# Another slot table for the side work of an attention kernel: two fills in one step, flags and values of a group later, norms' exponential one step earlier

## The chip, the cores and the metric

The kernel runs on one core of one Trainium2 chip. The metric is device time in microseconds of one execution, as the median of several runs. The profile is one further execution, recorded by the hardware.

## What is computed

Input is x of 8 batches x 1024 tokens x 256 features, and the layer has 16 heads of 16. Its reference, cut down:

```
x = x + attn(layernorm(x));  x = x + ffn(layernorm(x))
def attn(x):
    q, k, v = split_heads(x @ W_q.T), split_heads(x @ W_k.T), split_heads(x @ W_v.T)
    q_h, k_h, v_h = exp_map_at_origin(q, c), exp_map_at_origin(k, c), exp_map_at_origin(v, c)
    diff = |q_h|^2 - 2 q_h.k_h + |k_h|^2
    arg = maximum(1 + 2 c diff / ((1 - c |q_h|^2) (1 - c |k_h|^2)), 1 + EPS)
    weights = softmax(-beta * arccosh(arg) / sqrt(c) - bias)
    out = weights @ log_map_at_origin(v_h, c)
    out = log_map_at_origin(exp_map_at_origin(out, c), c)
    return concat_heads(out) @ W_o.T
def ffn(x):          # bfloat16 in; x and kernel rounded to float8_e4m3
    return bf16(f8(x / s_in) @ f8(kernel / s_k) * s_in * s_k) + bias
```

For each pair of a query and a key there is one logarithm and one power, 134 million of each (8 x 16 x 1024 x 1024).

## The kernel before

**Groups and steps.** The 8192 tokens are 16 groups of 512 query tokens (two groups per batch). For one group and one head group (4 of the 16 heads), the keys of the batch are run through in 8 tiles of 128. Such a piece is a step; a group has 32 steps (s = 0 to 31), the whole kernel 512 (n). In a step TensorE makes the `distances` of 128 keys x 512 queries x 4 heads as products of rows of 18 numbers (q_T, k_T) into four PSUM banks, ScalarE takes a logarithm of them (`log`, L1217) and an exponential of that (`power`, L1224), and TensorE multiplies by the values (`values`, into bank 6). Some groups of steps are "open": flags tell that a bound may be missed, and VectorE then computes and clamps (L1285, L1294). TensorE works ahead: in iteration n it issues the second half of the distances of step n+1 and the first half of n+2 (eight instructions, L1100), then side work, then the values of n-1, then more side work.

**Side work.** Besides the steps each group of tokens is projected once, two groups ahead, and finished once, one group after its steps. The projection of a group (`project_stage`) reads x, normalises it (xt), turns it (X, 2 fills), multiplies by the weights (M, 8 fills, L401), squares and sums q, k, v, finds 1/norm with Newton rounds (L267 to L269), takes the norms' exponential on ScalarE (L529), makes the values (L598 to L604), scales the rows of queries and keys, turns them (R, 8 fills, L406) and makes the flags from their largest norms (A, 2 fills, L411 to L414, then L509 to L521 on VectorE). The finish of a group (`finish_stage`) turns its sums (T, W, L695), and after the second normalisation does the feed-forward product (Q, Y, L700, L706). The sums of each head group are turned too (S, `turn_sums`, at s = 2, 10, 18, 26).

**Bank 7.** Every fill of this side work goes through PSUM bank 7: TensorE fills it, VectorE (in a few places another engine) copies it away, and only then comes the next fill. TensorE waits for `b7_copied` ahead of a fill, VectorE for `b7_filled` ahead of a copy. What follows the waiting fill in TensorE's order waits with it.

**Order.** The place of each piece is written out in tables. `PROJECT_USES` and `FINISH_USES` give for each fill a slot and a half of the step (0 ahead of the values, 1 behind, `BOTH` split). Slot k of the projection of group n is step s = k - 4 of group n - 2 (slots 0 to 3 are steps 28 to 31 before it; group 2's are a little different, `SECOND_USES`; groups 0 and 1 are projected ahead of the steps and in the first steps, `FIRST_FILLS` and `FIRST_USES`). Slot k of the finish is step k of the group after. `vector(v, n, k)` of both stages holds VectorE's work of a slot; in a step VectorE does the copies of bank 7 first, then `copy_sums` (at s = 0, 8, 16, 24; L1300), then the slot work of the finish, then that of the projection. `project.scalar` holds the exponential. Steps without a fill get a dummy product on bank 7 (`keep_busy`, L1138), except step `BARE`. Every fourth step is a new unit: each engine loads a flag and branches to the open or closed form of four steps. SyncE issues the DMAs of a slot in its own order.

**Table before, per step** (of groups 1 to 13): X0 0, X1 1, S 2, M0 3, M1 4, M2 5, M3 6, bare 7, M4 8, M5 9, S 10, M6 11, M7 12, T0 13, T1 14, W0 15, W1 17, S 18, R0 21, R1 22, R2 and A0 23, R3 24, R4 25, S 26, R5 and A1 27, R6 28, R7 29, Q0 30, Y0 and Y1 31.

## Time and profile before

| | us |
|---|---|
| median of 3 runs | 1992.56 |
| lowest and highest | 1990.39, 1993.75 |
| the profiled execution | 1994.49 |
| its span | 1992.7 |
| a regular group of 32 steps, by its first logarithms | 115.13 |
| the first group | 137.96 |

The page gives for each engine its busy time: ScalarE 1869.9 us (94%), TensorE 1788.6 (90%), VectorE 1142.9 (57%). In the rows below, "PE" is TensorE, "PEld" its weight loads, "DVE" VectorE, "ACT" ScalarE. A row of the timeline begins with its start; "[0.50 <-PE ps L700]" behind it says that the engine stood idle 0.50 us ahead of it and what ended that. Two ScalarE instructions that follow each other overlap a little, so that the durations are longer than the distance of the starts (1.78 us).

### The profile page before, as it was taken

The numbers are of one execution on the slowest core, as the hardware profiler recorded it, in microseconds if no ns is written. First come the engines' busy times: TensorE is split into PE (matmuls) and PEld (weight loads), VectorE is DVE, ScalarE is ACT, GpSimd is POOL, SyncE is SP. The second block draws the span as 40 slices with busy tenths as digits, with TensorE's granted clock in tenths as the row PEclk, the third lists the DMA queues.
The fourth block names the chain that finished last, engine by engine and source line by source line (L and its number), as shares of the span: only waits on it lengthen the run. The fifth ranks groups of instructions, "written<-read, shape, count | busy, mean of one in ns | idle before, by whom it ended". The sixth has DMA issues, their size and how long they took to land.

```text
span 1992.7 us, 29554 instructions
## 1 busy us (share of the span) xinstructions
PE 1788.6 (90%) x10713; PEld 603.1 (30%) x10713; DVE 1142.9 (57%) x2825; ACT 1869.9 (94%) x1094; POOL 12.8 (1%) x35
## 2 busy tenths in 40 slices
PE   7988989989898798989998898998989899899897
PEld 4322222323232232322322223232322223233234
DVE  7454565655656656565656647565565656323436
ACT  4889999999999799999998999999999999999883
POOL 2000000000000000000000000000000000000000
PEclk9799999999999899999999899999999999999889
DMA  1314213141312213132040321314131131411110
GB/s 56 112 49 144 54 54 103 42 134 43 112 44 78 77 44 112 43 101 75 23 134 22 110 67 44 112 43 134 40 107 52 56 90 43 123 43 53 33 33 23
DMA packets 112953, 142.54 MB, mean 72 GB/s; under 512 B 35691, under 2 KB 61548, under 8 KB 112748
## 3 DMA queue, kind: packets, MB, share of 16 engines
q1 hardware_dynamic: 112748, 140.13, 22.6%
q8 instruction: 89, 1.46, 0.3%
q14 instruction: 116, 0.95, 0.2%
HBM read 85.07 MB, written 55.05 MB: 70 GB/s over the span
## 4 chain that ended last, share of the span: by engine, by line
ACT 54%; PE 24%; issue 14%; DVE 4%; ACTq 3%; DMA 0%; DVEq 0%; SPq 0%
ACT U L1217 28%; ACT U L1224 26%; PE ps L1100 8%; PE ps L401 6%; PE ps L1115 5%; ACTq L1265 2%; PE ps L695 2%; DVE U L1294 1%; PE ps L1138 1%; PE ps L406 1%; PE ps L1142 1%; DVE U L1285 1%; DVE rows L554 0%; DMA U<-in_L_attn_W_o_dram 0%; ACT e L529 0%
## 5 line engine op out<-in xcount | busy, mean ns | idle before, releaser
L1224 ACT ACTIVATE U<-U 128x2048 f32<-128x2048 f32 x512 | 997.1, 1949 | 0.3
L1217 ACT ACTIVATE U<-ps 128x2048 f32<-128x2048 f32 x500 | 955.7, 1911 | 35.5 <-PE ps L1100 31.6
L1100 PE MATMUL ps<-q_T,k_T 18*128 18x512 f32 x4096 | 632.5, 652 | 133.0 <-ACT U L1217 107.7
L1115 PE MATMUL ps<-U,vals 128*32 128x512 f32 x4096 | 560.4, 620 | 29.4 <-ACT U L1224 28.9
L1100 PEld LDWEIGHTS ps<-q_T,k_T 18*128 18x128 f32 x4096 | 195.9, 187 | 356.8 <-ACT U L1217 296.4
L401 PE MATMUL ps<-wT,xnT 128*128 128x384 f32 x512 | 232.0, 545 | 4.9 <-DVEq L1318 2.5
L490 DVE COPY qkv<-ps 128x384 f32<-128x384 f32 x112 | 62.4, 557 | 243.7 <-PE ps L401 243.6
L1115 PEld LDWEIGHTS ps<-U,vals 128*32 128x32 f32 x4096 | 81.7, 109 | 205.4 <-ACT U L1224 159.2
L401 PEld LDWEIGHTS ps<-wT,xnT 128*128 128x128 f32 x512 | 81.1, 194 | 197.0 <-issue 132.4
L1138 PE MATMUL ps<-woT,ident 128*128 128x256 f32 x340 | 121.8, 441 | 3.8 <-DVEq L1318 3.6
L406 PE MATMUL ps<-ident,rows 128*128 128x128 f32 x512 | 107.2, 308 | 4.9 <-DVE rows L554 2.4
L406 PEld LDWEIGHTS ps<-ident,rows 128*128 128x128 f32 x512 | 55.1, 146 | 176.4 <-issue 114.5
L1138 PEld LDWEIGHTS ps<-woT,ident 128*128 128x128 f32 x340 | 52.0, 193 | 145.2 <-issue 116.0
L1300 DVE COPY OTs<-ps 128x512 f32<-128x512 f32 x64 | 43.8, 684 | 88.0 <-PE ps L1115 75.3
L498 DVE COPY q_T<-ps 128x512 f32<-128x512 f32 x60 | 41.5, 691 | 90.9 <-PE ps L406 90.3
L500 DVE COPY k_T<-ps 128x512 f32<-128x512 f32 x60 | 41.5, 691 | 62.8 <-PE ps L406 60.8
L695 PE MATMUL ps<-woT,fi_ocT 128*128 128x256 f32 x240 | 68.6, 409 | 0.0
L1308 DVE TENSOR_REDUCE den<-ps 128x16 f32<-128x256 f32 x64 | 27.2, 424 | 58.2 <-PE ps L1124 57.2
L695 PEld LDWEIGHTS ps<-woT,fi_ocT 128*128 128x128 f32 x240 | 41.0, 191 | 51.8 <-issue 37.3
L723 DVE TENSOR_TENSOR fi_x<-fi_xt,ps 128x512 f32<-128x512 f32 x30 | 20.6, 688 | 61.9 <-PE ps L695 61.9
L587 DVE TENSOR_TENSOR sqr<-qkv 128x768 f32<-128x768 f32 x56 | 53.3, 953 | 2.4
L588 DVE TENSOR_REDUCE ss<-sqr 128x48 f32<-128x768 f32 x56 | 53.4, 953 | 1.9
(209 smaller groups left out, 1179.6 us busy)
## 6 DMA issues: line engine op xcount, KB each, us to landing
rqb<-q_scratch SPq DMA_DIRECT2D x64, 1024.0 KB, 5.6
q_scratch<-q_T SPq DMA_DIRECT2D x16, 1024.0 KB, 4.5
k_scratch<-k_T SPq DMA_DIRECT2D x16, 1024.0 KB, 6.8
v_scratch<-vals SPq DMA_DIRECT2D x16, 768.0 KB, 9.6
fi_xt<-in_L_attn_x_dram SPq DMA_DIRECT2D x17, 512.0 KB, 6.0
xt<-in_L_attn_x_dram SPq DMA_DIRECT2D x15, 512.0 KB, 6.7
...
```

The costliest lines, as they stand in the source:

```text
L401: ins = pe.matmul(bank[:, 0:384], xnT[:, dc, t * P:(t + 1) * P], g.wT[:, dc, half * 384:(half + 1) * 384], start=dc == 0, stop=dc == 1)
L406: ins = pe.transpose(bank[:, t * P:(t + 1) * P], rows[:, qk, t, hg * HPG:(hg + 1) * HPG, :].rearrange("p h r -> p (h r)"), g.ident[:, :])
L490: v.tensor_copy(qkv[:, t, 24 * half:24 * (half + 1), :].rearrange("p h d -> p (h d)"), bank[:, 0:384]).then_inc(a.b7_copied, 1)
L587: step(v.tensor_tensor(sqr[:, :], src, src, ALU.mult))
L588: step(v.tensor_reduce(ss[:, t, :], sqr[:, :].rearrange("p (h d) -> p h d", d=DH), AX.X, ALU.add))
L695: ins = pe.matmul(bank[:, a * D:(a + 1) * D], ocT[:, dc, t * P:(t + 1) * P], g.woT[:, dc, :], start=dc == 0, stop=dc == 1)
L1100: ins = pe.matmul(g.ps[:, 2 * pair + i, :], a.k_T[HB * h:HB * h + RD, b % 2, hg, kt * P:(kt + 1) * P], a.q_T[HB * h:HB * h + RD, G % 3, hg ...
L1115: ins = pe.matmul(g.ps[HB * h:HB * h + VW, 6, :], a.vals[:, b % 2, kt, (hg * HPG + h) // 2, DH * (h % 2):DH * (h % 2) + VW], U[:, n % RING ...
L1138: pe.matmul(g.ps[:, 7, 0:D], g.ident[:, :], g.woT[:, 0, :], start=True, stop=True)
L1217: act.activation(U[:, n % RING].rearrange("p b n -> p (b n)"), chunk(n), ACT.Ln, scale=-2.0 / EPS, bias=1.0).then_inc(freed, 1)
L1224: act.activation(U[:, n % RING], U[:, n % RING], ACT.Exp, scale=exponent).then_inc(exp_done, 1)
L1300: v.tensor_copy(OTs[:, :], g.ps[:, 6, :]).then_inc(ot_done, 1)
```

## The change

Of the numbers of the table, these are moved (in steps of groups 1 to 13): X0 and X1 both in step 0 (one in each half), M0 to step 1, M1 and M2 to steps 3 and 4, step 5 bare, M3 and M4 to 6 and 7, step 8 bare, R0 to R4 in steps 21 to 25, A0 from 23 to 26 (behind the sums), A1 from 27 to 30 (behind Q0). The squares go to slots 9, 12, 13, 16; the Newton rounds to 17, 18, 19 with one each (before: one with the first guess in 18, two in 19); the norms' exponential from slot 21 to 20 (step 17 to 16); the values from slot 20 to 35 (step 16 to 31); the queries' rows are scaled in slot 23, the keys' in 24; three slots of the finish and its last DMA move by one; step 16 loses its dummy product. In the last groups the slots of the projection are packed otherwise (`SHORT_SLOTS`).

At the head, only the rows of head group 0 (R4, R0 of group 0) are turned ahead of the steps; the other six, which ScalarE copied from banks 6 and 7, now pass bank 7 and VectorE in steps 3, 10, 12 and 17. The rows of the keys of group 1 lie in their own place (`keys1`), the values of group 1 are made in step 2, the queries of group 1 are scaled in step 18 (before: 3), the feed-forward weights (`vector_kernel`) in step 13 (before: 12). Queries are stored one head group at a time. Some dummy products are added ahead of the first steps. The core of the diff:

```
-PROJECT_SLOTS = 35
-FINISH_SLOTS = 34
-PROJECT_USES = {("X", 0): (4, BOTH), ("X", 1): (5, BOTH),
-                ("M", 0): (7, BOTH), ("M", 1): (8, BOTH), ("M", 2): (9, BOTH), ("M", 3): (10, BOTH),
-                ("M", 4): (12, BOTH), ("M", 5): (13, BOTH), ("M", 6): (15, BOTH), ("M", 7): (16, BOTH),
-                ("R", 0): (25, BOTH), ("R", 1): (26, BOTH), ("R", 2): (27, 0), ("A", 0): (27, 1),
-                ("R", 3): (28, BOTH), ("R", 4): (29, BOTH), ("R", 5): (31, 0), ("A", 1): (31, 1),
-                ("R", 6): (32, BOTH), ("R", 7): (33, BOTH)}
+PROJECT_SLOTS = 37
+FINISH_SLOTS = 35
+PROJECT_USES = {("X", 0): (4, 0), ("X", 1): (4, 1),
+                ("M", 0): (5, BOTH), ("M", 1): (7, BOTH), ("M", 2): (8, BOTH), ("M", 3): (10, BOTH),
+                ("M", 4): (11, BOTH), ("M", 5): (13, BOTH), ("M", 6): (15, BOTH), ("M", 7): (16, BOTH),
+                ("R", 0): (25, BOTH), ("R", 1): (26, BOTH), ("R", 2): (27, BOTH), ("R", 3): (28, BOTH),
+                ("R", 4): (29, BOTH), ("A", 0): (30, 1), ("R", 5): (31, BOTH), ("R", 6): (32, BOTH),
+                ("R", 7): (33, BOTH), ("A", 1): (34, 1)}
...
-BARE = 7
-SHORT_SLOTS = {23: (23, 24), 24: (25, 26), 25: (27, 28), 26: (29,), 27: (30, 31), 28: (32,), 29: (33,), 30: (), 31: ()}
+BARE = (5, 8, 16)
+SHORT_SLOTS = {18: (18, 21), 19: (19, 22), 20: (20, 23), 21: (24,), 22: (25,), 23: (26,), 24: (27,), 25: (28,),
+               26: (29,), 27: (30, 31, 32), 28: (33,), 29: (34,), 30: (), 31: ()}
...
-FIRST_USES = {("A", 0): (2, 0), ("R", 4): (2, 0), ("A", 1): (2, 0), ("R", 5): (3, BOTH), ("R", 6): (6, BOTH),
-              ("R", 7): (11, BOTH), ("R", 0): (14, BOTH), ("R", 1): (17, BOTH), ("R", 2): (19, BOTH),
-              ("R", 3): (20, BOTH)}
+
+FIRST_USES = {("A", 1, 0): (2, 0), ("R", 1, 4): (2, 0), ("A", 1, 1): (2, 0), ("R", 0, 1): (3, 0), ("R", 0, 5): (3, 1),
+              ("R", 1, 5): (6, BOTH), ("R", 0, 2): (10, 1), ("R", 0, 6): (12, BOTH), ("R", 1, 6): (14, BOTH),
+              ("R", 0, 3): (17, 0), ("R", 0, 7): (17, 1), ("R", 1, 7): (18, 1),
+              ("R", 1, 0): (19, BOTH), ("R", 1, 1): (20, BOTH), ("R", 1, 2): (21, BOTH), ("R", 1, 3): (22, BOTH)}
...
-SECOND_USES.update({("R", 0): (25, BOTH), ("R", 1): (26, BOTH), ("R", 2): (27, 0), ("A", 0): (27, 1), ("R", 3): (28, 0),
-                    ("R", 4): (28, 1), ("R", 5): (29, BOTH), ("R", 6): (30, 0), ("A", 1): (30, 1), ("R", 7): (31, BOTH)})
+SECOND_USES.update({("M", 3): (9, BOTH), ("R", 0): (25, BOTH), ("R", 1): (26, BOTH), ("R", 2): (27, 0), ("A", 0): (27, 1),
+                    ("R", 3): (28, 0), ("R", 4): (28, 1), ("R", 5): (29, BOTH), ("R", 6): (30, 0), ("A", 1): (30, 1),
+                    ("R", 7): (31, BOTH)})
...
-    OWN = {0: 9, 1: 10, 9: 2, 11: 2, 14: 2, 17: 3, 18: 4, 19: 6, 20: 2, 21: 6, 22: 5, 23: 4}
+    OWN = {0: 9, 1: 10, 9: 2, 12: 2, 13: 2, 16: 3, 17: 4, 18: 3, 19: 3, 21: 6, 22: 5, 23: 4}
...
-        if k == 34:
+        if k == 36:
             b, u = n // 2, n % 2
             toks = slice(u * GTOK, (u + 1) * GTOK)
             kts = slice(u * GT, (u + 1) * GT)
+            sp.wait_ge(a.b7_copied, uses.after(("R", n, 3 if n == 1 else 7)))
...
+    def store_queries(sp, hg):
+
+        if hg:
+            sp.wait_ge(a.b7_copied, uses.after(("R", 0, hg)))
+        else:
+            sp.wait_ge(p_copied, len(FIRST_FILLS))
+        sp.dma_start(g.q_d[0, :, hg, 0:GTOK], a.q_T[:, 0, hg]).then_inc(q_out, 16)
+        sp.wait_ge(q_out, 16 * (hg + 1))
...
-        if k == 21:
+        if k == 20:
             act.wait_ge(n_rdy, n + 1)
             act.activation(e[:, :, :], nrm[:, :, :], ACT.Exp, scale=g.M2SC).then_inc(e_rdy, 1)
...
+    def query_columns(v, step):
+        step.mark(v.tensor_copy(rows[:, 0, :, :, 17], tt[:, :, 0:H]))
+        step.mark(v.tensor_copy(rows[:, 0, :, :, 18], rp[:, :, 0:H]))
+
+    def first_queries(v):
+
+        step = Steps(v, c_steps, 0)
+        query_columns(v, step)
+        scale_rows(v, 1, (0,))
...
-        if k in (9, 11, 14, 17):
-            t = {9: 0, 11: 1, 14: 2, 17: 3}[k]
+        if k in (9, 12, 13, 16):
+            t = {9: 0, 12: 1, 13: 2, 16: 3}[k]
...
-        if k == 18:
+        if k == 17:
             root_guess(v, step, ss[:, :, :], y[:, :, :])
             newton(v, step, ss[:, :, :], y[:, :, :], y2[:, :, :], 1)
+        if k == 18:
+            newton(v, step, ss[:, :, :], y[:, :, :], y2[:, :, :], 1)
         if k == 19:
-            newton(v, step, ss[:, :, :], y[:, :, :], y2[:, :, :], 2)
+            newton(v, step, ss[:, :, :], y[:, :, :], y2[:, :, :], 1)
             v.tensor_tensor(nrm[:, :, :], ssqk, yqk, ALU.mult).then_inc(n_rdy, 1)
-        if k == 20:
+        if k == (31 if n == 2 else 35):
+            step = first or Steps(v, g_steps, 2 * (n - 1))
...
+            if n >= 2:
+                scale_rows(v, n, (0,))
         if k == 24:
-            scale_rows(v, n, (1, 0))
-        assert first or step.n == OWN.get(k, 0), (k, step.n)
+            scale_rows(v, n, (1,))
...
-    OWN = {3: 1, 4: 2, 6: 11, 21: 9, 22: 10, 23: 4, 24: 2, 25: 2, 28: 2, 32: 1}
+    OWN = {3: 1, 4: 2, 6: 11, 21: 9, 22: 10, 23: 4, 24: 2, 25: 2, 27: 2, 33: 1}
...
-        QUERY_STEP, KERNEL_STEP = 3, 12
+        VALUES_STEP, QUERY_STEP, KERNEL_STEP = 2, 18, 13
...
+                        keep_busy_again(0, 3)
+                    if (kind, n, i) == ("R", 0, 0):
+                        keep_busy_again(0, 2)
                     project.first_tensor(pe, j)
-                    if (kind, n, i) == ("R", 0, 0):
-                        project.first_largest(pe, 1)
-                        distances(0, 0)
-                        distances(0, 1)
-                        distances(1, 0)
-                        project.await_largest(pe)
+                project.first_largest(pe, 1)
+                keep_busy_again(0, 2)
+                distances(0, 0)
+                distances(0, 1)
+                distances(1, 0)
+                project.await_largest(pe)
                 for n in range(N):
                     G, s = n // STEPS, n % STEPS
-                    if n + 1 < N:
+                    if n + 1 < N and n != 3:
                         distances(n + 1, 1)
-                    if n != 2:
+                    if n == 2:
...
-                        keep_busy_again(7, 5)
+                    if n in (0, 1):
+                        keep_busy_again(7, 6)
...
+                        if n == VALUES_STEP:
+                            project.vector(v, 1, 35)
                         for m, k in projected(G, s):
                             project.vector(v, m, k)
                         if G == LAST:
                             finish.last_early(v, s)
                         if n == QUERY_STEP:
-                            project.scale_rows(v, 1, (0,))
+                            project.first_queries(v)
```

Two places of the order, first VectorE at the start of a group. The last rows of steps 30 and 31 and the beginning of step 0 (fi_xb is the copy of Q0, fi_xq that of Y0 and Y1, xnT that of X0, amx that of A1, opens the flags, vg and vals the values), before:

```order
L726 COPY fi_xb<-ps 128x1024
L580 TENSOR_SCALAR xt<-xt,mv,rstd 128x256 x4
L728 TENSOR_SCALAR fi_xq<-ps,sc 128x512 x2
L1370 UNCONDITIONAL_BRANCH
L1364 TENSOR_LOAD opens
```

and of the change:

```order
L763 COPY fi_xb<-ps 128x1024
L531 COPY amx<-ps 1x32
L535 TENSOR_TENSOR prod<-amx 1x16 x3
L538 TENSOR_REDUCE prod<-prod 1x4 x3
L543 TENSOR_SCALAR opens<-prod 1x4 x3
L612 TENSOR_SCALAR xt<-xt,mv,rstd 128x256 x4
L765 TENSOR_SCALAR fi_xq<-ps,sc 128x512 x2
L633 TENSOR_SCALAR vg<-y,sc 128x64
L634 TENSOR_SCALAR vg<-vg,sc 128x64
L639 TENSOR_TENSOR vals<-qkv,vg 128x32x16 x2
L1410 UNCONDITIONAL_BRANCH
L1404 TENSOR_LOAD opens
```

The flags of A1 stand between the copy of Q0 and the scaling of xt, and the values between the copies of Y and the end of the unit. TensorE at the same place, steps 30 to 0 (L1100 distances, L700 Q0, L1115 values, L706 Y, L397 X), before:

```order
L1100 MATMUL ps<-q_T,k_T 128x512 x4
L700 MATMUL ps<-ident_b,fi_xq 128x128 x4
L1115 MATMUL ps<-U,vals 32x512 x4
L700 MATMUL ps<-ident_b,fi_xq 128x128 x4
L1100 MATMUL ps<-q_T,k_T 128x512 x4
L706 MATMUL ps<-kq,fi_xb 128x256 x4
L1115 MATMUL ps<-U,vals 32x512 x4
L706 MATMUL ps<-kq,fi_xb 128x256 x4
L1100 MATMUL ps<-q_T,k_T 128x512 x4
L397 MATMUL ps<-ident,xt 128x128 x2
L1115 MATMUL ps<-U,vals 32x512 x4
L397 MATMUL ps<-ident,xt 128x128 x2
```

and of the change:

```order
L1140 MATMUL ps<-q_T,k_T 128x512 x4
L737 MATMUL ps<-ident_b,fi_xq 128x128 x4
L1153 MATMUL ps<-U,vals 32x512 x4
L737 MATMUL ps<-ident_b,fi_xq 128x128 x4
L436 MATMUL ps<-ident,amax_r 1x32
L1140 MATMUL ps<-q_T,k_T 128x512 x4
L743 MATMUL ps<-kq,fi_xb 128x256 x4
L1153 MATMUL ps<-U,vals 32x512 x4
L743 MATMUL ps<-kq,fi_xb 128x256 x4
L1140 MATMUL ps<-q_T,k_T 128x512 x4
L419 MATMUL ps<-ident,xt 128x128 x4
L1153 MATMUL ps<-U,vals 32x512 x4
```

A1's fill stands behind the second half of Q0 and ahead of the distances, and X0 is whole ahead of the values of step 0 instead of half of it. Then VectorE in step 15, before (fi_x is the copy of W0; the Newton rounds end in nrm, for which the exponential waits):

```order
L717 COPY fi_ocT<-ps 128x512
L261 TENSOR_SCALAR y<-ss 128x192
L267 TENSOR_TENSOR y<-y 128x192
L268 SCALAR_TENSOR_TENSOR y<-y,ss 128x192
L269 SCALAR_TENSOR_TENSOR y<-y 128x192
L723 TENSOR_TENSOR fi_x<-fi_xt,ps 128x512
L267 TENSOR_TENSOR y<-y 128x192
L268 SCALAR_TENSOR_TENSOR y<-y,ss 128x192
L269 SCALAR_TENSOR_TENSOR y<-y 128x192
L267 TENSOR_TENSOR y<-y 128x192
L268 SCALAR_TENSOR_TENSOR y<-y,ss 128x192
L269 SCALAR_TENSOR_TENSOR y<-y 128x192
```

and of the change:

```order
L754 COPY fi_ocT<-ps 128x512
L270 TENSOR_TENSOR y<-y 128x192
L271 SCALAR_TENSOR_TENSOR y<-y,ss 128x192
L272 SCALAR_TENSOR_TENSOR y<-y 128x192
L760 TENSOR_TENSOR fi_x<-fi_xt,ps 128x512
L270 TENSOR_TENSOR y<-y 128x192
L271 SCALAR_TENSOR_TENSOR y<-y,ss 128x192
L272 SCALAR_TENSOR_TENSOR y<-y 128x192
L630 TENSOR_TENSOR nrm<-ss,y 128x128
```

One round fewer stands between W0's copy and the norms.

## Rows read from the trace of the kernel before

**Rows 1.** The page, one group: busy, mean ns of one | idle before, releaser.

```profile
L1217 ACT ACTIVATE U<-ps 128x2048 f32<-128x2048 f32 x500 | 955.7, 1911 | 35.5 <-PE ps L1100 31.6
```

**Rows 2.** Timeline, group 2, steps 15 to 17: start, us, engine, line, operation.

```profile
359.73 1.92 ACT L1224 ACTIVATE U<-U 128x2048 f32<-128x2048 f32 x1
...
362.57 0.36 DVE L267 TENSOR_TENSOR y<-y 128x192 f32<-128x192 f32 x1
...
363.75 0.29 DVE L596 TENSOR_TENSOR nrm<-ss,y 128x128 f32<-128x128 f32 x1
...
365.38 0.39 ACT L529 ACTIVATE e<-nrm,sc 128x128 f32<-128x128 f32 x1
```

**Rows 3.** Timeline, steps 30 to 0 at the start of group 2.

```profile
298.63 0.69 DVE L726 COPY fi_xb<-ps 128x1024 bf16<-128x1024 bf16 x1 [0.50 <-PE ps L700]
...
299.23 1.37 DVE L580 TENSOR_SCALAR xt<-xt,mv,rstd 128x256 f32<-128x256 f32 x4
...
300.44 1.97 ACT L1217 ACTIVATE U<-ps 128x2048 f32<-128x2048 f32 x1
...
300.71 0.75 DVE L728 TENSOR_SCALAR fi_xq<-ps,sc 128x512 bf16<-128x512 f32 x1
...
301.69 0.61 PE L706 MATMUL ps<-kq,fi_xb 128*128 128x256 bf16 x4
...
302.45 1.24 PE L1100 MATMUL ps<-q_T,k_T 18*128 18x512 f32 x8 [0.16 <-ACT U L1217]
...
303.99 1.98 ACT L1217 ACTIVATE U<-ps 128x2048 f32<-128x2048 f32 x1
...
305.73 0.69 DVE L487 COPY xnT<-ps 128x512 f32<-128x512 f32 x1 [2.64 <-PE ps L397]
```

**Rows 4.** Timeline, VectorE: flags of a group; values of a group.

```profile
287.65 0.18 DVE L509 COPY amx<-ps 1x32 f32<-1x32 f32 x1 [0.46 <-PE ps L414]
...
288.69 0.30 DVE L521 TENSOR_SCALAR opens<-prod 1x4 int32<-1x4 f32 x3
...
144.75 0.24 DVE L598 TENSOR_SCALAR vg<-y,sc 128x64 f32<-128x64 f32 x1
...
146.53 0.22 DVE L610 TENSOR_SCALAR rp<-e 128x128 f32<-128x128 f32 x1
```

**Rows 5.** Waits of the whole run: engine line, releaser: us in total, times, longest.

```profile
DVE OTs L1300 <- issue: 12.7, 13, 1.1
```

**Rows 6.** Timeline, group 1, step 26: distances; VectorE behind the sums.

```profile
284.63 1.24 PE L1100 MATMUL ps<-q_T,k_T 18*128 18x512 f32 x8 [0.70 <-ACT U L1217]
285.14 1.23 DVE L773 TENSOR_TENSOR fi_xq<-fi_ocT,fi_osq 128x1024 bf16<-128x1024 f32 x1
```

**Rows 7.** Timeline, ScalarE: logarithms of steps 4 and 7 of group 2.

```profile
318.22 2.01 ACT L1217 ACTIVATE U<-ps 128x2048 f32<-128x2048 f32 x1
...
329.43 1.88 ACT L1217 ACTIVATE U<-ps 128x2048 f32<-128x2048 f32 x1
```

**Rows 8.** Waits, 98:112, 160:176, 1925:1945 us; then the timeline of `vector_kernel`.

```profile
ACT U L1217 <- PE ps L1100: 5.9, 1, 5.9
...
ACT U L1217 <- PE ps L1100: 3.8, 2, 3.0
...
ACT U L1217 <- PE ps L1100: 4.0, 3, 1.9
...
115.86 0.48 DVE L235 TENSOR_SCALAR fi_osq<-fi_xb,sc 128x512 f32<-128x512 bf16 x1
...
119.94 0.56 DVE L490 COPY qkv<-ps 128x384 f32<-128x384 f32 x1
```

**Rows 9.** Timeline, TensorE: two R fills; busy time by stretch (behind POOL the clock).

```profile
160.60 0.41 PE L406 MATMUL ps<-ident,rows 128*128 128x128 f32 x2 [1.23 <-DVE rows L554]
...
165.75 0.44 PE L406 MATMUL ps<-ident,rows 128*128 128x128 f32 x2 [1.72 <-DVEq L1318]
...
168.00:170.00 2.00, 2.00 (x9) 0.52 (x8) 0.69 (x1) 0.00 (x0) 0.00 (x0) 0.50 0.03 8
```

More of the change, by code:

```diff
@@ L359, in pool_zero @@
         assert step.n == ZEROED
+        pool.wait_ge(reduced, 2 * GT)
+        step(pool.memset(keys1[:, :, :, DH:], 0.0))
+        step(pool.memset(keys1[:, :, :, 17:18], -1.0))
     ZEROED = 4 + NS
@@ L538, in first_vector @@
         step(v.tensor_scalar(ss[:, :, :], ss[:, :, :], EPS * EPS, None, ALU.max))
-        vector(v, n, 18, step)
-        vector(v, n, 19, step)
+        for k in (17, 18, 19):
+            vector(v, n, k, step)
         if n == 0:
             v.wait_ge(zeroed, ZEROED)
-        vector(v, n, 20, step)
+            vector(v, n, 35, step)
         vector(v, n, 21, step)
@@ L965, in in_step @@
             if G == 0:
-                found += [(kind, 1, i) for kind, i in at(FIRST_USES, s, half)]
+                found += at(FIRST_USES, s, half)
             return found
@@ L1238, in unit @@
                             power(n - 1, freed)
-                        if not is_open and n == 0:
-                            other_copies()
-                            project.scalar(act, 1, 21)
+                        if not is_open and n == 1:
+                            project.scalar(act, 1, 20)
                         if not is_open and n == n0:
```

82 lines of the change are left out of this document (42 added, 40 removed).

## The prediction

> **What bounds the kernel now.** I start with the groups of instructions. ScalarE runs two activations per step, logarithm and power, over 512 steps, and the logarithm is idle 35.5 us in all, nearly all of it behind the distances of TensorE [rows 1]. Then the timeline of a regular stretch: a logarithm begins every 3.56 us (300.44 to 303.99 [rows 3]); a group of 32 steps takes 115.13 us by its first logarithms, 1.2 us over 32 such steps. ScalarE sets the time, and TensorE, VectorE and the single PSUM bank 7 matter only where one of them is late for a logarithm. So each edit has one question: is a logarithm kept waiting that was not? Three places of a group are near it: the start of the group (side work for two groups passes bank 7), step 17 (the exponential of the norms stands between two logarithms), and steps 4 to 6 (fill after fill of bank 7). Last I read the head (steps 0 to 31), where most of the present loss sits, and the granted clock.
>
> **Part 1: the start of a group.** Before, Q0, Y0, Y1, X0, X1 take bank 7 in steps 30, 31, 31, 0, 1. Q's copy starts at 298.63, VectorE scales xt from 299.23, and copies Y0 at 300.71. The distances at 302.45 then come 0.3 us early for the logarithm of 303.99 [rows 3]. In the changed kernel A1 fills bank 7 behind the second half of Q0, in the same step. TensorE stands in order: A1's fill has to wait for Q0's copy (to 299.3), with the distances of the next logarithm queued behind it, 0.3 us late. VectorE then does the flags of A1, which take 1.5 us from the copy to the last flag (287.65, 288.69 and 0.3, with small gaps [rows 4]; I take 1.48) before the xt scaling (1.48: 299.23 to 300.71 [rows 3]). So Y0's copy comes at 302.55 and not at 300.71. Y1's fill waits for it until 303.35 (before: 301.69 [rows 3]), and the next distances stand behind Y1: 303.35 + 0.6 (Y1) + 1.2 (eight distances, 1.24 [rows 3]) = 305.1 against 303.99, so +1.1.
> Y1's copy ends at 304.8. Now the values of the slot moved from 20 to 35 follow on VectorE, 1.86 us (144.75 to 146.53, with the next start [rows 4]), then the start of a four-step unit, 1.1 us [rows 5], and only then X0's copy: 307.75 against 305.73 before [rows 3]. X1 now stands in the same step, its fill waits for that copy (308.45), and the distances behind it end at 308.45 + 0.44 + 1.24 = 310.1; this logarithm began at 307.55, so **+2.6**. The following two steps add 0.3, M1 and M2 in steps 3 and 4 add 0.4, and then the old chain of four M fills in steps 3 to 6, which cost 0.53 (318.22 to 329.43 is 11.21 for three steps of 3.56 [rows 7]), is gone, since step 5 is bare: **+2.8 per group start**. The rest, ScalarE at its pace, can't win that back. Twelve full starts: 33.6; group 14's (only the finish) 1.1, group 1's 1.0. Together **+35.7**. Bounds: 0 if VectorE runs ahead of Q0 (then A1 costs nothing), +4.7 per start if the M fills keep their old loss and each copy is 1 us later.
> Beside this, a rule. Rows 5 show 1.1 us ahead of the first copy of a unit, which holds a load of a flag and a branch. The Trainium skill ("Advanced Engine Details and Errata", section "Control Flow Timing") gives a branch about 50 ns and a compare-and-branch about 110 ns. By those prices X0's copy would come near 1 us earlier, an estimate from that page, and the total some 11 us lower; the trace does not agree, and nothing else here uses it.
>
> **Part 2: the exponential.** Before, the norms are ready at 363.75 + 0.29 = 364.04, and ScalarE reaches its exponential at 365.38, no wait [rows 2]. The change puts the exponential one step earlier, behind the power that starts at 359.73; ScalarE is free for it at 359.73 + 1.8 = 361.5. VectorE has one Newton round less at that place (the round from 362.57 to 363.75 [rows 2]; it moved to slot 18, with another), so the norms are ready at 362.57 + 0.29 = 362.9. ScalarE stands 1.4 us with nothing else it may do: the next logarithm is queued behind the wait, and for it the distances. I take 0.15 off, which is won back from small waits of the steps around it (a group holds 1.2 us of waits in all, the 0.53 of part 1 among them): **+1.25 each, 13 groups, +16.3**. Bounds: 0 and 1.7. It would be 0 if the first W fill came a whole step earlier, but that does not move.
>
> **Part 3: A0 behind the sums.** Step 26 now has the sums (S) and A0. A0's fill waits for VectorE's copy of the sums, which is done when the next instruction starts at 285.14; the distances stood at 284.63 [rows 6]. They start at 285.3 and 0.26 of that is over ScalarE's lead: 13 x 0.26 = **+3.4**. (Bounds 0 and 9.) Key and query scaling apart (slots 23, 24), squares one slot on, stores later, `scaled` and `rmax` one slot earlier: all lie beside ScalarE's work with whole steps of room, so nothing. The new zeroing on Pool and the per-head-group stores on SP: also nothing, since neither queue holds up a step after the first.
>
> **Part 4: head and tail.** One logarithm waits 5.9 us in steps 10 and 11 of group 0, where the sums and a chain of M fills collide [rows 8]. M3 of group 2 moves from slot 10 to 9: -5.0. `vector_kernel` moves from step 12 to 13, behind the copy of M5 and its squares; it holds VectorE from 115.86 to 119.94, 4.1 us [rows 8], and a fill of bank 7 waits for it: +2.6. The queries of group 1 are scaled in step 18 and not in step 3, with the norms' exponential in front of them; three R fills (steps 17, 18, 19) want them: +4.8, an estimate between 0 and two such blocks of VectorE (8.2). The start itself: six copies fewer on ScalarE ahead of the second step, but more fills and padding ahead of the first logarithm: +1 (0 to +4). Steps 25 to 28: -0.7. One further stretch of low clock: about +2.3. **Head +5.** Group 5 (an open unit): -0.5. Tail: three waits of 4.0 us in all stood in the last group, where Q0 meets the finish [rows 8]; the earlier short slots take these and a little of the end after the last step: **-4.4**.
>
> **Part 5: the clock.** Ahead of the R fill at 165.75 TensorE stood idle for 1.72 us, and at 168 to 170 the granted clock is 0.50, the lower of its two levels (1.2 instead of 2.4 GHz); the idle 1.23 us ahead of 160.60 had no such sequel [rows 9]. In the cold stretch ScalarE waits 3.8 us in two places [rows 8]. My stalls leave TensorE idle for up to 1.5 to 2.3 us at some points of a group. In most of these it keeps a filled bank ahead; I take 3 cold stretches of 3.3 us in the regular groups, **+10** (bounds 0 and 26 of them).
>
> **Sum.** 35.7 + 16.3 + 3.4 + 5 - 0.5 - 4.4 + 10 = +65.5 against the profiled execution's 1994.5 (its span is 1992.7, and 1.8 us lie around it), so 2060. The median of the runs is 1.9 below that execution: **2058**.
>
> **Rivals.**
> Both stalls exist but only one decides (0.20). VectorE is 57% busy and could be ahead of TensorE at the group's start; then A1 and Y0 are copied early and the start costs under 1 us. For: before the change each wait for VectorE there is short. Against: the order on VectorE is fixed and there is nothing to skip. With only the exponential: 16.3 + 3.4 + 12 (12 starts of 1) - 5 (head, tail) = +27 or, with only the starts, +40: **2010 to 2032**.
> The clock falls in the new idle places in most groups (0.15). For: 1.7 us of idle stood ahead of a fall. Against: 1.2 us stood ahead of none [rows 9]. 13 to 26 cold stretches of 3.3 us instead of 3: **2092 to 2135**.
> The other side: faster (0.10). The deciding point is VectorE's lead: if it stands at least 1.5 us further ahead at steps 15 and 30 than I placed it, neither stall reaches a logarithm, since ScalarE has no other new wait. What stays is the gain of the table: the M chain's 0.53 in 12 groups (6.4), the collision in the head (5.0) and the tail (4.4), less 0 to 3 for the queries. 1992.6 - 15 = **1976 to 1985**. Against it: the first of the two stalls is read from instructions whose places I know to 0.1 us.
>
> **How the numbers follow.** My forecast (starts +2.8, exponential +1.25, few cold stretches) has 0.53, with its own range of 2040 to 2080: cold stretches 0 or 8, head 0 to +10. One stall 0.20, cold 0.15, faster 0.10, within 0.2% 0.02 (gain and loss cancel). The measurement can tell about 0.2% from no change. The range leaves out the faster case and the upper part of the cold one, 2 in 10: 2002 to 2095. Faster 0.10, same 0.02, slower 0.88.
>
> **What would show it.** ScalarE's exponential of the norms in a regular group is preceded by idle of about 1.4 us, released by VectorE's norms: right for part 2; no idle there and part 2 is wrong. The first logarithms of a group stand 1.1 and 2.6 us later than a step of 3.56 would have them, with the distances as releaser and Y1's and X1's fill waiting for copies of VectorE: part 1. The intervals of steps 4 to 6 fall to 3.56. The 5.9 us in the head are gone. A regular group takes about 119.4 us (115.13 + 2.8 + 1.25 + 0.26). If it takes 116 or less the whole forecast is wrong; if over 121 the clock row tells which rival it is.

## The result, and the profile after

The changed kernel takes 2050.84 us (median of 6 runs, 2045.26 to 2057.92) against 1991.47 us of the kernel before in the same comparison (6 runs, 1984.75 to 1993.85): ratio 1.0306, 95% interval 1.0279 to 1.0333, 59 us slower. The forecast was 2058, within 2002 to 2095. The profiled execution of the changed kernel was its fastest (2045.26 us, span 2043.4), so the two traces differ by 50.7 us and not by 59. A "cold stretch" below is a stretch in which the granted clock of TensorE is 0.50.

The group of the logarithms on the page (busy, mean ns | idle before, releaser), which answers to [rows 1]:

```profile
L1257 ACT ACTIVATE U<-ps 128x2048 f32<-128x2048 f32 x500 | 944.6, 1889 | 70.1 <-PE ps L1140 61.3
```

Idle ahead of the logarithms has doubled, from 35.5 to 70.1 us, 61.3 of it behind the distances. Work did not grow: ScalarE's and VectorE's busy times are the same to 3 us, and TensorE's is 15 us less (its dummy products fell from 139.8 to 121.1 us). A second wait is new, from the waits of the whole run (total us, times, longest):

```profile
ACT e L551 <- DVE nrm L630: 21.2, 16, 3.0
```

From the starts of the logarithms in both timelines I took the interval of every step; the regular groups lose at three places. (Group 3, us from one logarithm to the next; the other steps are 3.55 to 3.59 in both.)

| step | before | after | what stands there |
|---|---|---|---|
| 31, 0, 1 | 3.56, 3.56, 3.56 | 3.59, 3.88, 4.04 | Q0, A1, Y, X on bank 7 |
| 2 | 3.56 | 3.75 | sums, M fills |
| 4, 5, 6, 7 | 3.56, 3.71, 3.75, 3.75 | 3.66, 3.75, 3.57, 3.56 | M fills |
| 16, 17 | 3.82, 3.87 | 5.22, 3.56 | norms' exponential |
| 18 | 3.65 | 5.40 | sums, W1 |
| 27 | 3.56 | 3.84 | A0 behind the sums |

**The exponential** (timeline of group 3, steps 16 and 17, which answers to [rows 2]):

```profile
488.11 1.07 PE L1153 MATMUL ps<-U,vals 128*32 128x512 f32 x8
...
488.96 0.29 DVE L630 TENSOR_TENSOR nrm<-ss,y 128x128 f32<-128x128 f32 x1
489.29 0.40 ACT L551 ACTIVATE e<-nrm,sc 128x128 f32<-128x128 f32 x1 [1.24 <-DVE nrm L630]
489.60 1.86 ACT L1257 ACTIVATE U<-ps 128x2048 f32<-128x2048 f32 x1
...
491.51 0.81 PE L1140 MATMUL ps<-q_T,k_T 18*128 18x512 f32 x4 [2.34 <-ACT U L1257]
```

ScalarE stands idle 1.24 us until the norms are there; the next logarithm is queued behind that, and TensorE, whose next distances need a bank that this logarithm frees, is idle for 2.34 us. What comes after is in the busy times by stretch of the same group (PE, PEld, DVE, ACT, POOL; the number behind POOL is the granted clock), one microsecond a row:

```profile
491.80:492.80 1.00, 1.00 (x9) 0.24 (x7) 0.00 (x0) 1.00 (x1) 0.00 (x0) 1.00 0.00 0
492.80:493.80 1.00, 1.00 (x4) 0.70 (x4) 0.00 (x0) 1.00 (x2) 0.00 (x0) 0.69 0.00 0
493.80:494.80 1.00, 1.00 (x6) 0.20 (x8) 0.00 (x0) 1.00 (x1) 0.00 (x0) 0.50 0.00 0
494.80:495.80 1.00, 1.00 (x8) 0.00 (x0) 0.00 (x0) 1.00 (x2) 0.00 (x0) 0.50 0.00 0
495.80:496.80 1.00, 1.00 (x6) 0.66 (x3) 0.00 (x0) 1.00 (x1) 0.00 (x0) 0.60 0.00 0
496.80:497.80 1.00, 1.00 (x8) 0.54 (x10) 0.31 (x1) 0.02 (x1) 0.00 (x0) 1.00 0.00 0
```

The clock falls to its lower level (0.50) after TensorE has begun again, stays there about 3 us, and ScalarE runs dry in the last row (ACT 0.02): that is the 5.40 of step 18. It is so in 11 of the 13 groups 1 to 13; in the kernel before, none of these groups has a cold stretch in these steps. Groups 1 and 7 had the same idle stretch of 2.34 us and kept a full clock; their step 18 takes 3.81 and 3.82. Four groups had a longer cold stretch, and their step 18 takes 6.72 to 7.04.

**The start of a group** (timeline, group 3, which answers to [rows 3]; L743 fills Y, L419 X, L436 A1, and L763, L765, L509 are the copies of Q0, Y and X):

```profile
424.12 0.69 DVE L763 COPY fi_xb<-ps 128x1024 bf16<-128x1024 bf16 x1 [0.99 <-PE ps L737]
...
424.86 0.18 PE L436 MATMUL ps<-ident,amax_r 32*1 32x32 f32 x1 [0.86 <-DVE fi_xb L763]
...
425.09 0.18 DVE L531 COPY amx<-ps 1x32 f32<-1x32 f32 x1 [0.28 <-PE ps L436]
...
425.80 0.16 DVE L543 TENSOR_SCALAR opens<-prod 1x4 int32<-1x4 f32 x1
...
426.11 1.38 DVE L612 TENSOR_SCALAR xt<-xt,mv,rstd 128x256 f32<-128x256 f32 x4
...
427.41 0.74 DVE L765 TENSOR_SCALAR fi_xq<-ps,sc 128x512 bf16<-128x512 f32 x1
...
428.21 0.61 PE L743 MATMUL ps<-kq,fi_xb 128*128 128x256 bf16 x4 [0.56 <-DVE fi_xq L765]
...
429.92 1.88 ACT L1257 ACTIVATE U<-ps 128x2048 f32<-128x2048 f32 x1 [0.21 <-PE ps L1140]
430.09 1.29 DVE L639 TENSOR_TENSOR vals<-qkv,vg 128x512 f32<-128x512 f32 x2
...
431.46 0.69 DVE L509 COPY xnT<-ps 128x512 f32<-128x512 f32 x1
...
432.20 0.66 PE L419 MATMUL ps<-ident,xt 128*128 128x128 f32 x4 [0.73 <-DVE xnT L509]
...
433.96 1.88 ACT L1257 ACTIVATE U<-ps 128x2048 f32<-128x2048 f32 x1 [0.36 <-PE ps L1140]
```

The chain is the one that was forecast, Q0, A1, flags, Y, values, X, but shorter. Between the logarithm of 422.45 and Y0's copy there are 4.96 us (forecast 5.67, before 3.83); at the starts of even groups it is 5.43 to 5.74. X0's copy begins at once behind the values at all twelve starts.

Summed over the two traces (differences of group times by first logarithms), the 50.7 us are: steps 16 to 18 without the cold stretches 13 x 1.26 = 16.4; cold stretches behind them 24, and two in step 28 1.7; starts of groups 1 to 13 (steps 31 to 7, the M chain included) 11.7, about 1.3 in even groups and 0.8 in odd ones, less 0.4 in group 1; step 27 3.7; head 2.4 (group 0 takes 142.72 and not 137.96, its first logarithm comes 2.4 earlier); last group and end -9.1; that leaves -0.1. In the last group 4.4 us are steps 26 to 28, which fell from 5.65, 4.93 and 4.46 to 3.56 each. Another 5.1 are cold stretches that the profiled execution of before had in steps 8 to 13 and the one of after had not; 1.7 of that is lost again in step 16, where the one of after had a cold stretch.

### The profile page after: what moved, and what is told of

It reads as the page before. It is cut to its first block, busy times and chain, and to the rows that moved or that the text cites. A ratio compares the mean times of both kernels' runs of the same rounds, so it can differ in the third digit from the quotient of the medians.

```text
span 2043.4 us, 29504 instructions
## 1 busy us (share of the span) xinstructions
PE 1774.0 (87%) x10681; PEld 597.0 (29%) x10681; DVE 1144.1 (56%) x2831; ACT 1872.4 (92%) x1088; POOL 14.2 (1%) x37
## 4 chain that ended last, share of the span: by engine, by line
ACT 41%; PE 25%; issue 16%; DVE 15%; ACTq 2%; DVEq 1%; DMA 0%; SPq 0%
ACT U L1264 21%; ACT U L1257 19%; PE ps L1140 7%; PE ps L1153 6%; PE ps L423 4%; PE ps L732 4%; ACTq L1303 2%; PE ps L1180 1%; DVE U L1332 1%; DVE fi_x L819 1%; DVE xt L612 1%; DVE fi_xq L765 1%; PE ps L428 1%; DVE fi_ocT L808 1%; DVE on L1350 1%
## 5 line engine op out<-in xcount | busy, mean ns | idle before, releaser
L1257 ACT ACTIVATE U<-ps 128x2048 f32<-128x2048 f32 x500 | 944.6, 1889 | 70.1 <-PE ps L1140 61.3
L1264 ACT ACTIVATE U<-U 128x2048 f32<-128x2048 f32 x512 | 984.8, 1925 | 0.3
L1140 PE MATMUL ps<-q_T,k_T 18*128 18x512 f32 x4096 | 626.6, 648 | 149.6 <-ACT U L1257 122.1
L1176 PE MATMUL ps<-woT,ident 128*128 128x256 f32 x264 | 92.5, 433 | 3.5 <-DVEq L1356 3.5
L732 PE MATMUL ps<-woT,fi_ocT 128*128 128x256 f32 x240 | 81.3, 469 | 0.0
L1176 PEld LDWEIGHTS ps<-woT,ident 128*128 128x128 f32 x264 | 39.5, 188 | 110.4 <-issue 93.1
L732 PEld LDWEIGHTS ps<-woT,fi_ocT 128*128 128x128 f32 x240 | 48.1, 223 | 65.9 <-issue 50.4
L1252 ACT ACTIVATE U<-U 128x2048 f32<-128x2048 f32 x12 | 22.9, 1912 | 26.8 <-DVE U L1332 26.7
```

The lines of the kernel that those rows point to most:

```text
L732: ins = pe.matmul(bank[:, a * D:(a + 1) * D], ocT[:, dc, t * P:(t + 1) * P], g.woT[:, dc, :], start=dc == 0, stop=dc == 1)
L1140: ins = pe.matmul(g.ps[:, 2 * pair + i, :], a.k_T[HB * h:HB * h + RD, b % 2, hg, kt * P:(kt + 1) * P], a.q_T[HB * h:HB * h + RD, G % 3, hg ...
L1176: pe.matmul(g.ps[:, 7, 0:D], g.ident[:, :], g.woT[:, 0, :], start=True, stop=True)
L1257: act.activation(U[:, n % RING].rearrange("p b n -> p (b n)"), chunk(n), ACT.Ln, scale=-2.0 / EPS, bias=1.0).then_inc(freed, 1)
L1264: act.activation(U[:, n % RING], U[:, n % RING], ACT.Exp, scale=exponent).then_inc(exp_done, 1)
```

## The experiments

Every kernel was compared with the kernel before on the same chip. Times are medians, with the ratio to that kernel and its interval where it decides. Between experiments the chips differ; the median of the kernel before was 1988.1 to 1992.0 us in them.

**1. The exponential back in slot 21.**

```
-        if k == 20:
+        if k == (21 if n >= 2 else 20):
```

> The changed kernel with only the norms' exponential of groups 2 and later back in slot 21 (step 17). Theory (the wait for the norms costs 1.4 us, leaves TensorE idle about 2.3 us, and that idle stretch is what the clock falls after): ScalarE waits nothing at the exponential, steps 16 to 18 fall from 5.22 + 3.56 + 3.8 (5.4 or 7.0 in most groups) to 3.8 + 3.9 + 3.65, and the granted clock is 1.00 in steps 16 to 18 of all groups: 16 us of waits and 23 us of cold stretches go, 2051 to about 2011. Rival (the clock falls because step 16 has no dummy product, or for another reason in these steps): only the 16 us go, about 2035, and step 18 keeps 5.4 in most groups.

Measured: 2014.13 us, ratio 1.0117 (1.0082 to 1.0153). Steps 16 and 17 are 3.82 and 3.87 in groups 1 to 13 and step 18 is 3.56. 37 us have gone, forecast 40. So the wait and the clock's falls in steps 17 and 18 go together. The missing dummy product alone does not bring the falls about: step 16 still had none here, TensorE stood idle 0.96 us in it, and the clock fell in none of the 13 groups (timeline, group 3):

```profile
490.95 1.24 PE L1140 MATMUL ps<-q_T,k_T 18*128 18x512 f32 x8 [0.96 <-ACT U L1257]
...
492.60 0.39 ACT L551 ACTIVATE e<-nrm,sc 128x128 f32<-128x128 f32 x1
```

**2. The dummy product of step 16 back, the wait kept.**

```
-BARE = (5, 8, 16)
+BARE = (5, 8)
```

> The changed kernel with only the dummy product of step 16 put back (BARE = (5, 8)). Theory (the idle stretch of TensorE decides the clock): ScalarE's wait stays, step 16 stays at 5.22, but TensorE's idle stretch is about 0.7 us shorter and the clock falls in fewer groups, so that step 18 is 3.8 in most of them: 2051 to about 2031. Rival (the stretch is still long enough, 2.3 - 0.7 = 1.6 us): 2050, step 18 at 5.4 or 7.0 as before.

Measured: 2030.79 us, ratio 1.0212 (1.0182 to 1.0242), 20 us less than the changed kernel. Step 16 stays at 5.22 to 5.23, and step 18 is 3.81 or 3.82 in 11 of 13 groups and 5.40 in the other two. The idle stretch was 1.09 us and not the 1.6 I expected, since two dummy products stand in the step (timeline, group 3):

```profile
485.24 0.40 ACT L551 ACTIVATE e<-nrm,sc 128x128 f32<-128x128 f32 x1 [1.24 <-DVE nrm L630]
...
487.45 1.24 PE L1140 MATMUL ps<-q_T,k_T 18*128 18x512 f32 x8 [1.09 <-ACT U L1257]
```

**3. Twice as many dummy products there.**

```
                     if unused:
                         keep_busy(first_use[n])
+                        if s == 16:
+                            keep_busy_again(7, 1)
```

(the same behind the values, and `BARE` as in 2)

> The changed kernel with the dummy products of step 16 put back and doubled (two behind the distances, two behind the values). Theory (the longer TensorE's idle stretch at the exponential, the more often the clock falls: 2.34 us, 11 of 13 groups; 1.09 us, 2 of 13): the stretch is under 0.5 us, no group of 13 has a cold step 18 (3.8 everywhere), step 16 stays at 5.22: 2031 to about 2029. Rival (the falls are not set by this stretch): 2 or more of 13 groups keep 5.4 in step 18.

Measured: 2027.09 us, ratio 1.0190 (1.0166 to 1.0214). The idle stretch is 0.22 us, step 16 still 5.22, and step 18 is 3.81 or 3.82 in all 13 groups. TensorE in group 3:

```profile
491.87 0.70 PE L1176 MATMUL ps<-woT,ident 128*128 128x256 f32 x2
492.41 0.59 PE L1180 MATMUL ps<-woT,ident 128*128 128x256 f32 x2
493.22 1.24 PE L1140 MATMUL ps<-q_T,k_T 18*128 18x512 f32 x8 [0.22 <-ACT U L1261]
```

The wait of ScalarE is the same in the three kernels; TensorE's idle stretch is 2.34, 1.09 and 0.22 us, and the clock fell in 11, 2 and 0 of 13 groups. The dummy products shorten the idle stretch and add work at once; which of the two counts is not separated here. The wait itself costs what it cost.

**4. The same edit in the kernel before**: `scalar` in slot 20, one Newton round each in slots 17, 18 and 19; the dummy products of step 16 stay.

> The kernel before with only the norms' exponential of groups 2 and later in slot 20 and the Newton rounds in slots 17, 18, 19 (one each, the first with the guess); step 16 keeps its dummy products. Theory (the wait for the norms belongs to this one edit): 13 x 1.26 us for the wait in step 16 (5.22 instead of 3.82) and at most three cold stretches of 1.6 us, since the dummy products hold TensorE's idle stretch at 1.1 us: 1990 to about 2009. Rival (the rest of the new table brings the wait about, and not this edit): 1990, step 16 at 3.8.

Measured: 2017.62 us, ratio 1.0135 (1.0105 to 1.0166), 28 us slower than before, forecast 19. Step 16 is 5.40 and not 5.22, so that steps 16 to 18 cost 1.4 more and not 1.26; and here four groups of 13 fell at an idle stretch of 1.09 us. 13 x 1.42 + 4 x 1.6 is 25 us, and the profiled execution is 25.1 longer than that of the kernel before; the other 3 us between the medians are not accounted for. The one edit makes the wait, with none of the rest of the table.

**5. The values back in slot 20** (`if k == (20 if n >= 2 else 35)`).

> The changed kernel with only the values of groups 2 and later back in slot 20 (step 16). They hold VectorE 1.86 us in step 31, ahead of the copy of X0. Theory (that copy, which comes at once behind the values, is what X1's fill and the distances of the second step wait for): step 1 falls from 3.88 to 4.03 to about 3.6, at most 0.5 in each of 12 groups, 2051 to about 2045. Rival (the fill of X0 comes too late anyway, because X0 and X1 stand in one step): no change, 2051, step 1 as before.

Measured: 2048.6 us with a wide spread (2032.99 to 2054.71), so that the time decides nothing between 2045 and 2051. The trace does: step 1, which had been 3.88 to 4.04, is 3.57 in groups 2 to 13, step 0 keeps 3.88 in odd groups and about 4.35 in even ones, and the groups' times less the cold stretches fall by 0.3 to 0.9. So the values make step 1 late, and not the two X fills in one step. Cold stretches were in 8 of 13 groups, at the same idle stretch of 2.34, and they make the spread: the four executions of 2033.0, 2045.3, 2051.9 and 2054.7 us had a mean granted clock of 0.974, 0.964, 0.960 and 0.958.

**6. The flags back**: A0 in step 23, A1 in step 27.

```
+                ("R", 0): (25, BOTH), ("R", 1): (26, BOTH), ("R", 2): (27, 0), ("A", 0): (27, 1), ("R", 3): (28, BOTH),
+                ("R", 4): (29, BOTH), ("R", 5): (31, 0), ("A", 1): (31, 1), ("R", 6): (32, BOTH),
+                ("R", 7): (33, BOTH)}
```

> The changed kernel with only A0 and A1 back in steps 23 and 27, each in the second half of a step whose R fill stands in the first half. Theory (A0 behind the sums costs 0.28 us per group, A1 behind Q0 keeps Y0's copy back by its flags, 1.0 us in odd groups and 1.5 us in even ones): step 27 falls from 3.84 to 3.56 and step 0 from 3.88 (odd groups) and 4.35 (even groups) to 3.6; 13 x 0.28 and 12 x 0.55 go, 2051 to about 2041. Rival (the values in step 31, not the flags, hold the start back): only the 3.7 us, 2047, step 0 as before.

Measured: 2046.89 us. Steps 27, 31, 0 and also 1 are 3.56 in all groups: with Y0 copied in time even the values no longer hold X0's copy. That is most of 11.7 + 3.7, but only 4 us are seen. In its trace 10 of 13 groups had a cold stretch, and seven of these were long (step 18 at 6.4 to 6.7, where most had been 5.40), 27 us in place of 24; and groups 0 and 14 took 149.0 and 124.0 us, where they had taken 142.7 and 114.6. How long a cold stretch lasts goes with when the clock falls. In the five kernels here that have this wait and such falls, 12 falls set in between 0.25 us before TensorE's new start and 0.51 us after it; these stretches lasted about 7 us and cost 3.0 to 3.2. The other 23 set in 0.76 to 1.99 us after it, lasted about 3 us and cost 1.6. In this kernel the long ones are the more frequent. Here the clock is down before TensorE starts (timeline and busy time by stretch, group 3):

```profile
497.51 2.19 PE L1140 MATMUL ps<-q_T,k_T 18*128 18x512 f32 x8 [2.34 <-ACT U L1257]
...
496.50:497.50 1.00, 0.00 (x0) 0.00 (x0) 0.27 (x1) 1.00 (x2) 0.00 (x0) 0.99 0.00 0
497.50:498.50 1.00, 0.98 (x4) 0.62 (x8) 0.00 (x0) 1.00 (x1) 0.00 (x0) 0.50 0.00 0
```

**7. All three put back**, with the new slots of X and M, the new head and tail.

> The changed kernel with the exponential in slot 21, the values in slot 20 and A0 and A1 in steps 23 and 27, as before the change, all for groups 2 and later; the slots of X and M, the head and the tail stay as the change has them. Theory (these three places hold all that the regular groups lost): a regular group takes 115.1 us, 13 groups x 4 to 6 us go, 2051 to about 1995; what is left against the kernel before is the head (+5 to +9 with a cold stretch there) less the tail (-4). Rival (each fix alone leaves idle stretches of TensorE in other places that the clock falls after): regular groups over 116 us, above 2005.

Measured: 1993.31 us (10 runs), ratio 1.0013 (1.0000 to 1.0026). Regular groups take 114.77 us, less than the 115.13 of before. So the three places hold the whole loss of the regular groups, and what was gained there and in the tail is given back in group 0, which takes 149.60.

**8. Only the new slots of X and M, in the kernel before.**

> The kernel before with only the new slots of X0, X1 and M0 to M7 for groups 3 and later (both X fills in step 0, M0 in step 1, M1 and M2 in 3 and 4, steps 5 and 8 bare). Theory (X0 and X1 in one step cost nothing where no flags and no values stand ahead of them on VectorE, and the new places of the M fills only move the small waits): steps 0 and 1 stay at 3.56, steps 2, 4 and 5 lose 0.2, 0.1 and 0.2 instead of 0.15, 0.2 and 0.2 in steps 5 to 7, so no change, 1990. Rival (two fills in step 0 are themselves too many): 0.3 or more in step 1, 12 groups, 1994 or more.

Measured: 1983.27 us (10 runs), ratio 0.9964 (0.9945 to 0.9983): a little faster than before. Steps 6 and 7 fall from 3.75 to 3.57 and 3.56, and nothing rises, 0.37 us a group. I had taken the new M places from the changed kernel, where step 2 is 3.75; that 0.19 too belonged to the late X, and without it step 2 is 3.56.

**9. Only the new slots of the finish and the packed last group, in the kernel before.**

> The kernel before with only the new slots of the finish (8 to 7, 28 to 27, 32 to 33, its last DMA 33 to 34) and the new packed slots of the last group. Theory (the tail's gain is that Q0 no longer waits for VectorE in steps 26 to 28 of the last group): these three steps fall from 5.65, 4.93 and 4.46 to 3.56, 4.4 us less, 1990 to about 1985. Rival (most of the 8 us by which the last group is shorter is a cold stretch that one execution had and the other not): the time within 2 us of before.

Measured: 1991.5 us, ratio 1.0014 (1.0000 to 1.0028), no gain. Steps 26 to 28 of the last group are 3.56, as forecast, -4.4; but step 10 of every regular group is 4.00 to 4.34, where 3.58 stood. On VectorE, at the start of the unit of step 8:

```profile
326.98 0.95 DVE L589 TENSOR_REDUCE ss<-sqr 128x48 f32<-128x768 f32 x1
...
329.52 0.56 DVE L491 COPY qkv<-ps 128x384 f32<-128x384 f32 x1 [1.59 <-issue]
...
330.13 0.91 PE L402 MATMUL ps<-wT,xnT 128*128 128x384 f32 x2 [0.69 <-DVE qkv L491]
...
333.99 1.88 ACT L1218 ACTIVATE U<-ps 128x2048 f32<-128x2048 f32 x1 [0.67 <-PE ps L1101]
```

`scaled` now stands ahead of the start of that unit and no longer behind it, and the copy that releases the next M fill comes 1.59 us after the squares.

**10. X, M and the tail together, without `scaled`'s move.**

> The kernel before with only the new slots of X and M (groups 3 and later) and the new packed slots of the last group; of the finish's moved slots all but the one from 8 to 7. It has the head, the flags, the values, the exponential and the squares of the kernel before. Theory (head, flags, values and exponential are what the change loses by; the rest gains): the 4.4 us of the tail and the 0.36 us per regular group add up, 1983 to about 1979, and 1993 (all three places put back, new head) less this, 14 us, is the price of the head. Rival (slot 8 to 7 of the finish is needed with the new M slots, or 28 to 27 costs what the tail gains): 1983 or more.

Measured: 1983.69 us, ratio 0.9973 (0.9957 to 0.9989). Regular groups take 114.87, the last one 117.38, but groups 5 and 8 take 131.26 and 128.48 where experiment 8 has 130.60 and 126.53. The tail's gain is eaten by the two open groups (2.6 us), 0.1 us in each regular group, and a step 10 of group 14 that takes 4.73. Against the 1993.31 of experiment 7 it is 9.6 us, the head and what goes with it; I had expected 14.

**11. `KERNEL_STEP` 12 in the kernel of experiment 7.**

> The kernel with all three places put back and the new head, with only the feed-forward weights' step 13 put back to 12. Theory (in step 13 they stand behind squares and hold the copy of R3 that releases the next M fill; TensorE stands idle 3 us there and its clock falls): step 16 of group 0 falls from 8.9 to under 6, 1993 to about 1989. Rival (the block of 4 us on VectorE costs the same one step earlier): 1993, another step of group 0 takes the wait.

Measured: 1988.09 us (ratio 0.9987, 0.9974 to 1.0001), 5 us less. Step 16 of group 0 falls from 8.9 to 3.8, and step 15 rises from 3.6 to 6.3: the block costs 2.7 where it cost 5.3. The rival was half right. In the changed kernel the block is seen like this (timeline of group 0):

```profile
117.33 0.69 DVE L241 TENSOR_TENSOR kq<-fi_osq 128x512 bf16<-128x512 f32 x1
...
118.06 0.69 DVE L522 COPY k_T<-ps 128x512 f32<-128x512 f32 x1
118.80 1.65 PE L423 MATMUL ps<-wT,xnT 128*128 128x384 f32 x2 [3.06 <-DVE k_T L522]
...
125.34 1.88 ACT L1257 ACTIVATE U<-ps 128x2048 f32<-128x2048 f32 x1 [5.53 <-PE ps L1140]
```

An M fill (two matmuls in 1.65 us, where two take 0.91 at full clock) waits 3.06 us for the copy behind the block and then runs cold.

**12. X, M and the packed last group, every finish slot as before.**

> The kernel before with the new slots of X and M for groups 3 and later and only the packed slots of the last group; every slot of the finish in the other groups stays as it was. Theory (the moved slots of the finish cost a regular group 0.1 us and groups 5 and 8 some 2 us, which ate the tail's gain in the version that had both): regular groups at 114.77 us, steps 26 to 28 of the last group at 3.56, 1983 to about 1979. Rival (the tail's gain of 4.4 us in steps 26 to 28 is only the logarithms' and not the end's, since the last group's sums are late anyway): 1983.

Measured: 1974.35 us (6 runs, 1973.06 to 1983.1) against 1991.96, ratio 0.9929 (0.9908 to 0.9951), the fastest of all. Regular groups 114.77, group 5 130.61, group 8 126.53, the last group 115.80, steps 26 to 28 at 3.56: the moved finish slots had eaten the tail's gain. The logarithms' idle time is 18.4 us:

```profile
L1219 ACT ACTIVATE U<-ps 128x2048 f32<-128x2048 f32 x500 | 957.2, 1914 | 18.4 <-PE ps L1102 16.8
```

Its median is 9 us below experiment 8, where the traces account for 4.4. The rest goes with how many executions had more cold stretches. Seven of experiment 8's ten had a mean granted clock of 0.972 to 0.978 and took 1982.7 to 1990.2 us, the other three 0.982 and 1974.4 to 1977.2; here five of six had 0.980 to 0.984 and took 1973.1 to 1975.1, and one had 0.976 and took 1983.1. The kernel before has the same two kinds: of 61 executions 22 at 0.976 or 0.977 took 1984.1 to 1986.8, 25 at 0.972 or 0.973 took 1989.3 to 1994.4, and 14 lay between. Compared kind with kind this kernel gains some 9 to 11 us, and not the 17.6 of the medians; that the new slots also make the cold stretches rarer is not shown by six runs. Of the six traces with the head of before, three have group 0 at 130.7 to 130.8 and three at 137.9, 138.0 and 141.6.

## Why the prediction was right, and where it was not

The time came out 7 us from the forecast, and that is partly luck: two terms were wrong by more than that, the starts by 24 us too much and the clock by 16 us too little, and they happened to cancel. The sign that was named for it, a regular group of about 119.4 us, came out by the same luck: groups with a short cold stretch take 119.0 to 119.8, but with the cold stretches taken off groups 2 to 13 take 117.4 to 118.2 (open groups left out).

**Part 2, the exponential: right.** Forecast +1.25 a group over steps 16 to 18, measured 1.26 (5.22 + 3.56 + 3.82 against 3.82 + 3.87 + 3.65). Both ends were in the trace of before: when ScalarE would be free, and when the round ahead of the norms ended. Their difference was 1.4, and the 0.15 taken off was an allowance, so the second decimal is chance: the same edit in the kernel before cost 1.42. Experiments 1 and 4 show the cause from both sides.

**Part 3, A0: right.** +0.26 forecast, +0.28 measured in step 27 in 12 of 13 groups, and gone in experiment 6.

**Part 1, the start: right chain, wrong size.** Forecast +2.8 a start, measured about 1.3 in even groups and 0.8 in odd ones; 35.7 forecast, 11.7 measured. Two terms failed. First, the flags: I took the chain of even groups for all, but at the starts of odd groups each of the three operations is one instruction and not three (from the copy at 425.09 to the scaling at 426.11 are 1.0 us, not 1.48). Second and larger, the 1.1 us of a unit's start was put behind the values [rows 5]. In the trace X0's copy begins 0.08 us after the values end (430.09 + 1.29 = 431.38, copy 431.46). That row of before holds 13 starts, one a group, where VectorE had nothing left to do behind the norms; with the values still running, the load of the flag and the branch passed beside them (430.20 to 430.89 in the trace of group 3) and cost nothing. So X0's copy, and with it X1's fill, came 1.9 us earlier than forecast in group 3, and step 1 lost 0.3 to 0.5 and not 1.5. The Trainium skill gives about 51 ns for a branch and 108 ns for a compare-and-branch ("Advanced Engine Details and Errata", "Control Flow Timing"). By an estimate from these the copy would have come about 1 us earlier than by my sum. The trace agrees on the copy; but experiment 9 has 1.59 us of idle ahead of a copy at another unit's start, far more than those prices.

The rival in which only one stall decides (0.20) had 12 starts of 1 us, and that is nearly what was measured, though VectorE did not run ahead as it supposed; its total failed on the clock. It also took 5 us off for head and tail, where the forecast's own terms give 0.

**Part 5, the clock: right mechanism, wrong count.** Forecast 3 cold stretches at 3.3 us, +10. Measured 13 in groups 1 to 13 (11 in step 18, two in step 28), for 26 us: four long ones at 3.2 each, seven short ones at 1.6 and two at 0.8. I had reasoned that most idle places would be shorter than the 1.7 us of [rows 9], and put the exponential's at "1.5 to 2.3" without asking which end; it was 2.34, in each group. The rival of the falling clock (0.15) was thus right on the number of stretches (13 to 26), and its price of 3.3 us holds for the long ones alone; had the start cost what I forecast, the sum would have been 24 us higher.

**Part 4, head and tail.** Steps 26 to 28 of the last group gave -4.4, as forecast. The head was forecast at +5. The two traces give +2.4, but other executions of the same head give more: group 0 took 142.7 to 149.6 us in eight traces with the new head and 130.7 to 141.6 in six with the old, and experiment 7 against 10 gives 9.6 us in the medians. The start itself, forecast at +1, gained instead: the second logarithm begins at 48.12 us and not at 55.45, because the six row copies and an exponential no longer stand on ScalarE between the first two. Most of it is lost again in steps 1 to 4. `vector_kernel` cost 5.3 with its cold stretch in experiment 7 (5.65 in the changed kernel), where I had 2.6 + 2.3 in two separate terms; steps 17 to 21, for which I had +4.8, lost 5.8. And one wait was missed altogether, 3.8 us in step 4: a copy of R1 stands behind the values of group 1 and the normalisation of group 2's tokens.

```profile
70.06 0.69 DVE L520 COPY q_T<-ps 128x512 f32<-128x512 f32 x1
...
70.81 1.12 PE L428 MATMUL ps<-ident,rows 128*128 128x128 f32 x4 [3.39 <-DVE q_T L520]
...
73.98 1.88 ACT L1257 ACTIVATE U<-ps 128x2048 f32<-128x2048 f32 x1 [5.27 <-PE ps L1140]
```

The six row copies that ScalarE had done between the first two logarithms now stand in VectorE's order, behind such blocks. And the -5.0 for the collision in steps 10 and 11 was partly a cold stretch: in traces without one the old kernel needs 6.9 in step 11 and not 9.6, and the new one 4.8.

**Also missed:** that the new places of the X and M fills in themselves make the kernel a little faster (experiment 8), and that moving the finish's slots costs the open groups and step 10 (experiments 9 and 10). For the first I had a gain of 0.53 and a loss of 0.4 a group, where experiment 8 shows a gain of 0.37; the second I had set at nothing. The intervals of steps 4 and 5 did not fall to 3.56, as a sign of the forecast had it, but are 3.66 and 3.75. The faster rival's upper end, 1985, does not follow from its terms, which give 1977 to 1980.
